# Partial sums of the middle token stages added in DRAM by POOL's transfers, rests copied out by ACT, seven-product blocks of 512 columns, first weight slots in other buffers

## Chip, cores and metric

One core of one Trainium2 chip (trn2). The metric is the device time of one execution in microseconds, from three executions of the kernel before: 2330.68 (median), 2330.60 and 2334.85.

## What is computed

The inputs are x (32 x 128 x 2048, fp32) and the weights of two layers of which the second follows the first. Cut to what matters:

```python
# layer 1: weight [2048, 2048] + low-rank part, quantised by groups of 128 to a 32-level codebook
lora_delta = lora_B @ lora_A * 0.5
normalized = (weight + lora_delta).reshape(2048, 16, 128) / exp(scale_log)
quantized  = cb[searchsorted((cb[:-1] + cb[1:]) * 0.5, normalized)]
w_eff      = (quantized * scale).reshape(2048, 2048) + lora_delta
y = x @ w_eff.T
# layer 2: a base matrix, a rank-16 part mixed by a softmax over 8 experts
result = y @ W_base.T + b_base
ax, probs = y @ A_w.T, softmax(y @ router_w.T)
mixed  = einsum(ax, cores, probs)
return x + result + mixed @ B_w.T * 2
```

The kernel never forms y. It multiplies w_eff with [W_base; A_w; router_w] first (2048 x 2072), and x with that product.

## The kernel before

The 16 blocks of 128 rows of the contraction are taken in four groups of four, g = 0 to 3. For each group there is a **weight stage**, in which TensorE multiplies the quantised weight with the wide second matrix and leaves the product in SBUF as a high and a low part (`gh`, `gl`, 2072 columns each), and then a **token stage**, in which all 32 tokens (t, tiles of 128 rows of x) are multiplied with it. Every fp32 factor is held as a rounded high part and a remainder, and each product is three matmuls (high x high, high x low, low x high). Beside all of it a background of quantisation "levels" for the later groups runs on ACT (masks `mk` and `mp`), DVE (`acc`) and POOL (`tm`, `pp`).

Four token stages add to the same 32 x 128 x 2072 result, which does not fit into SBUF. It lies in DRAM as `part`, one tile of 1,036 KB for each token, and three SBUF buffers `R.part[t % 3]` hold what is in work.

The change is in the **middle token stages, g = 1 and g = 2**. There tokens are taken in pairs p = 0 to 15. The first and the last pair are plain: for each token five "chunks" of 384, 384, 384, 512 and 408 columns, 12 matmuls each. The 14 pairs between are "mixed": the first `SW` = 448 columns of both halves of the result (`HX` = 1036 columns each) come from a scheme with seven products instead of eight (`prod` 1 to 7, 6 matmuls of `SW` columns each), and the remaining columns of each token are three "rest" units (12 matmuls of `REST` columns each). The thirteen units of a mixed pair run in this order:

```python
MIX = (("prod", 1), ("prod", 2), ("rest", 0, 0), ("rest", 0, 1), ("prod", 6), ("prod", 5), ("rest", 0, 2), ("prod", 7),
       ("prod", 3), ("rest", 1, 0), ("prod", 4), ("rest", 1, 1), ("rest", 1, 2))
```

Positions in a pair are counted by this list, 0 to 12 (`at` in the code). The products alternate between two PSUM banks (`unit_bank`), the rests go round four others. TensorE waits in `mul` until the unit that used its bank before has been taken out.

The generator `walk` yields all events in one order, and each engine's program picks its own from it, so the order of an engine's instructions is fixed by the places of the `yield`s; each engine then waits on semaphores alone. In the middle stages of the kernel before:

- SP (the queue of all transfers) loads the tokens' x (`load_x`, L872 to L883) at position 0 for both tokens of the next pair, loads each token's old partial sum from DRAM into `R.part[t % 3]` (`load_part`, L890) once the store of token t - 3 has landed (semaphores `po`), and stores it back (`store_part`, L901) when DVE has added the last unit of it. It is one queue: what waits holds up what stands behind.
- DVE takes every unit out of PSUM by adding it to the loaded buffer (`mul_added`, L1743 to L1761), which waits for the load (`pi`) once for each token.
- ACT rounds x to its high part (`split_x`, L1505) and POOL subtracts to get the low part (`split_x`, L2038), for the even token at position 5 and the odd token at position 7. POOL also forms the sums of x blocks for the next pair (`token_sums`, L2056 to L2061), which ACT rounds (L1517) and DVE finishes (L1769).
- The weights of the next weight stage come in small slots (`weight`, L852 to L870). The first six are asked for at position 6 of the last pair. Four of them lie in the `part` buffers, and wait for the last stores from these (`po`).

## Time and profile before

| | us |
|---|---|
| median of three executions | 2330.68 |
| the other two | 2330.60, 2334.85 |
| the profiled execution, its own time | 2334.6 |
| its span, first to last instruction | 2331.3 |
| PE busy in the span | 2252.6 (97%) |
| DVE / ACT / POOL busy | 1952.5 / 1495.4 / 1391.5 |
| mean granted TensorE clock | 0.992 |

The stages follow each other in the span like this: token stage g = 1 from 891.6 to 1244.5 us, weight stage g = 2 to 1426.9, token stage g = 2 to 1776.0, then the weight and token stage of g = 3. "Busy" of PE counts a matmul from its start to a modelled end, and consecutive matmuls overlap: the time that a matmul costs is read from the distance of two starts, not from its duration.

### The profile page before, as it was taken

What the parts mean: (1) busy time and instruction counts of PE and PEld (TensorE: products, weight loads), DVE (VectorE), ACT (ScalarE), POOL (GpSimd) and SP (SyncE); (2) the same over time, 40 slices, a digit from 0 to 9 for tenths busy, and PEclk for the clock granted to TensorE, in tenths of its full rate; (3) what the DMA queues carried; (4) which work ended last, traced back from release to release, by engine and by line L of the source; (5) the groups of instructions that cost most, each with busy time, mean ns of one, the idle gap of its engine ahead of it and who ended that gap; (6) DMA issues with size and microseconds to landing.
All of it is one profiled execution on the core that took longest, in us unless ns stands there. A gap on an engine that the chain in (4) does not pass through costs nothing.

```text
span 2331.3 us, 31903 instructions
## 1 busy us (share of the span) xinstructions
PE 2252.6 (97%) x11610; PEld 2061.2 (88%) x11610; DVE 1952.5 (84%) x2501; ACT 1495.4 (64%) x1962; POOL 1391.5 (60%) x902
## 2 busy tenths in 40 slices
PE   3989899999999999999999999999999999999999
PEld 2445479999999989999999989999999999999998
DVE  8999998889988977989997988999996766777676
ACT  7999978989877764666664865666663664121221
POOL 6888846669874545878775635988872132233331
PEclk9999999999999999999999999999999999999999
DMA  6787854444334334656664334566656666656454
GB/s 209 260 288 272 315 208 170 163 170 145 133 128 149 116 109 169 254 214 240 248 231 153 115 109 167 221 244 246 234 223 195 187 193 192 226 192 235 189 222 154
DMA packets 133233, 459.62 MB, mean 197 GB/s; under 512 B 14114, under 2 KB 66914, under 8 KB 96354
## 3 DMA queue, kind: packets, MB, share of 16 engines
q1 hardware_dynamic: 133076, 457.59, 56.1%
q8 instruction: 91, 1.49, 0.3%
q14 instruction: 66, 0.54, 0.1%
HBM read 306.41 MB, written 151.13 MB: 196 GB/s over the span
## 4 chain that ended last, share of the span: by engine, by line
PE 80%; DVE 8%; DMA 4%; ACT 3%; POOL 2%; issue 2%; SPq 0%; DVEq 0%; POOLq 0%; ACTq 0%
PE m L1228 6%; PE m L1227 6%; PE m L1229 6%; PE m L1179 5%; PE m L1180 5%; PE m L1181 5%; DVE acc L1701 5%; PE m L1120 5%; PE m L1334 4%; PE m L1336 4%; PE m L1335 4%; PE m L1294 3%; PE m L1293 3%; PE m L1295 3%; PE m L1284 3%; PE m L1285 2%
## 5 line engine op out<-in xcount | busy, mean ns | idle before, releaser
L1701 DVE SCALAR_TENSOR_TENSOR acc<-mk,dj,acc 128x1024 f32<-128x1024 uint8 x736 | 944.4, 1283 | 91.4 <-ACT mk L1449 73.2
L1449 ACT ACTIVATE mk<-wr,bj 128x1024 uint8<-128x1024 f32 x736 | 811.1, 1139 | 0.5 <-DVE acc L1701 0.4
L2014 POOL TENSOR_TENSOR pp<-pp,tm 128x1024 f32<-128x1024 f32 x184 | 456.9, 2483 | 22.9 <-POOL tm L2000 1.5
L2000 POOL TENSOR_SCALAR tm<-mp,dj 128x1024 f32<-128x1024 uint8 x192 | 225.8, 1177 | 219.8 <-ACT mp L1455 213.0
L1799 DVE TENSOR_TENSOR kl<-kw,kh 128x416 fp32r<-128x416 f32 (+3 forms) x310 | 240.5, 785 | 84.5 <-ACT kh L1484 83.5
L1484 ACT ACTIVATE kh<-kw 128x416 fp32r<-128x416 f32 (+3 forms) x310 | 169.1, 548 | 183.2 <-DMA kw<-in_wb 91.9
L1228 PE MATMUL m<-gl,xh 128*128 128x384 f32 (+2 forms) x800 | 280.9, 351 | 0.0
L1227 PE MATMUL m<-gh,xh 128*128 128x384 f32 (+2 forms) x800 | 280.6, 351 | 0.0
L1229 PE MATMUL m<-gh,xl 128*128 128x384 f32 (+2 forms) x800 | 279.9, 350 | 0.0
L1455 ACT ACTIVATE mp<-wr,bj 128x1024 uint8<-128x1024 f32 x224 | 255.0, 1139 | 13.7 <-POOL wr L1980 13.7
L1761 DVE TENSOR_TENSOR part<-m,part 128x448 f32<-128x448 f32 (+4 forms) x362 | 210.8, 593 | 34.1 <-PE m L1229 16.7
L1179 PE MATMUL m<-kh,wh 128*128 128x384 f32 (+2 forms) x624 | 219.3, 351 | 0.6 <-DVE part L1761 0.6
L1181 PE MATMUL m<-kh,wl 128*128 128x384 f32 (+2 forms) x624 | 218.6, 350 | 0.0
L1180 PE MATMUL m<-kl,wh 128*128 128x384 f32 (+2 forms) x624 | 218.6, 350 | 0.0
L1120 PE MATMUL m<-rows,wr 128*128 128x384 f32 (+2 forms) x560 | 208.3, 535 | 2.6 <-DMA rows<-in_wb 2.2
L1120 PEld LDWEIGHTS m<-rows,wr 128*128 128x128 f32 x560 | 112.5, 201 | 97.3 <-issue 51.5
L1840 DVE TENSOR_TENSOR part<-m,part 128x346 f32<-128x346 f32 (+1 forms) x272 | 137.1, 516 | 69.3 <-PE m L1336 36.0
L1334 PE MATMUL m<-op,pxh 128*128 128x346 f32 (+1 forms) x544 | 178.8, 329 | 0.0
L1335 PE MATMUL m<-op,pxh 128*128 128x346 f32 (+1 forms) x544 | 174.3, 320 | 0.0
L1293 PE MATMUL m<-gh,xh 128*128 128x392 f32 x504 | 171.8, 341 | 2.3 <-DVE part L1761 2.3
L1294 PE MATMUL m<-gl,xh 128*128 128x392 f32 x504 | 171.8, 341 | 0.0
L1295 PE MATMUL m<-gh,xl 128*128 128x392 f32 x504 | 171.4, 340 | 0.0
(249 smaller groups left out, 5140.8 us busy)
## 6 DMA issues: line engine op xcount, KB each, us to landing
part<-part SPq DMA_DIRECT2D x191, 1036.0 KB, 4.8
rows<-in_wb SPq DMA_DIRECT2D x61, 1036.0 KB, 4.8
out<-part SPq DMA_DIRECT2D x31, 1024.0 KB, 4.8
kw<-in_ws SPq DMA_DIRECT2D x128, 208.0 KB, 2.7
xw<-in_x SPq DMA_DIRECT2D x96, 256.0 KB, 5.1
kw<-in_wb SPq DMA_DIRECT2D x92, 192.0 KB, 2.4
wr<-in_w SPq DMA_DIRECT2D x32, 512.0 KB, 5.8
dl<-delta SPq DMA_DIRECT2D x30, 512.0 KB, 5.4
```

The costliest lines, as they stand in the source:

```text
L1120: done = e.matmul(R.m[c][:, 0:width(c)], R.wr[raw_of(q)][:, (t % 8) * 128:(t % 8 + 1) * 128], R.rows[r % 3][:, cols(c)], start=t == 0, sto ...
L1179: e.matmul(bank[:, 0:w], high, kh, start=t == 0, stop=False)
L1180: e.matmul(bank[:, 0:w], high, kl, start=False, stop=False)
L1181: done = e.matmul(bank[:, 0:w], low, kh, start=False, stop=t == NB - 1 and not own(b, c))
L1227: e.matmul(R.m[c][:, 0:w], xh, gh, start=k == 0, stop=False)
L1228: e.matmul(R.m[c][:, 0:w], xh, gl, start=False, stop=False)
L1229: done = e.matmul(R.m[c][:, 0:w], xl, gh, start=False, stop=stop and k == n - 1)
L1334: e.matmul(bank, high, oh, start=kp == 0 and n in (1, 2, 5), stop=False, skip_group_check=n in (3, 4, 6, 7))
L1335: e.matmul(bank, high, ol, start=False, stop=False, skip_group_check=n in (3, 4, 6, 7))
L1449: e.activation(R.mk[m % NM], w, ACT.Identity, bias=R.bj[:, j:j + 1], scale=GROW).then_inc(S["mk"], 1)
L1701: e.scalar_tensor_tensor(R.acc, R.mk[m % NM], R.dj[:, j:j + 1], R.acc, ALU.mult, ALU.add).then_inc(S["ac"], 1)
L2014: e.tensor_tensor(R.pp, first, R.tm[scaled_level(q, i)], ALU.add).then_inc(S["pp"], 1)
```

## The change

In the token stages g = 1 and g = 2:

1. **Partial sums.** `load_part` is gone, and `store_part` stays for g = 0 alone. A unit is now written into `R.part[t % 3]` by a copy, or, for the second and later product of the same target, added to what this pair has put there. When a token's last unit is out, POOL issues one transfer that adds the whole buffer to `part[t]` in DRAM (`add_part`; `accum_op=ALU.add`, rows in two pieces of 1036 elements). It stands at position 10 of the pair for the even token, and at position 1 of the next pair for the odd one. The first unit of token t waits until the transfer of token t - 3 has landed (semaphores `pa`).
2. **Who takes out.** ACT copies the rest units and chunks 0, 1, 2 (`mul_copied`); DVE takes out the products and chunks 3, 4 (`mul_evicted`).
3. **Low part of x.** For the odd tokens (beyond the first pair) it moves from POOL to DVE, and from position 7 to 10 (8 in plain pairs). The even token's x is asked for at position 8 of the pair before (`fetch_ahead`) instead of position 0 of the next.
4. **Columns.** `SW` goes from 448 to 512. The rests shrink from 392, 392 and 392 columns to 348, 348 and 352. To make room, the buffer `sf` of the x sums moves to the enlarged `las`.
5. **Weight slots.** For the weight stages g = 2 and g = 3 the first six slots, and slots 10 and 11, lie in `las`, in the four x buffers, and in freed places of the raw weights or `dl` (`GUESTS`). None of them waits for a transfer of partial sums.

The diff, cut to its core:

```diff
-GUEST = {4: 2, 5: 0}
-GUEST_LAST = {2: 0, 3: 1, 10: 0, 11: 1}
+GUESTS = {1: {4: "x2", 5: "x0"},
+          2: {0: "las", 1: "x0", 2: "x1", 3: "x2", 4: "sh", 5: "x3", 10: "las", 11: "sh"},
+          3: {0: "las", 1: "x0", 2: "x1", 3: "x2", 4: "sl", 5: "dl", 10: "sl", 11: "dl"}}
...
-SW = 448
+SW = 512
...
                 yield ("x_split", g, 2 * p + 3)
-                yield ("more", g, p)
...
-            if at == 7:
+            if at == (10 if mixed(p) else 8):
                 yield ("x_low", g, 2 * p + 3)
...
+        if at == (10 if mixed(p) else 6):
+            yield ("half_stored", g, p)
+        if p and at == 1:
+            yield ("pair_stored", g, p - 1)
+        if at == 8 and p + 2 < PAIRS:
+            yield ("fetch_ahead", g, 2 * p + 4)
...
-        elif s in GUEST:
-            e.wait_ge(S["mc"], x_released(g - 1, GUEST[s]))
+        place = GUESTS[g].get(s, "")
+        if place[:1] == "x":
+            e.wait_ge(S["mc"], x_released(g - 1, int(place[1])))
+        elif place == "las":
+            e.wait_ge(S["ql"], sums_count(g - 1, MIX_LAST))
+        elif place == "dl":
+            e.wait_ge(S["we"], NQ)
+        elif place:
+            e.wait_ge(S["mc"], sums_free(g - 1))
...
-    def load_part(g, t):
-        if t < 3:
-            e.wait_ge(S["used"], NS * (g - 1) + RELEASED[t])
-        else:
-            e.wait_ge(S[f"po{t % 3}"], slot_round(g, t - 3))
-        e.dma_start(R.part[t % 3], part[t]).then_inc(S[f"pi{t % 3}"], 16)
...
+    def mul_copied(g, k):
+        p, kind, u, i = UNITS_OF[g][k]
+        t = 2 * p + u
+        part, bank = R.part[t % 3], (*R.m, R.pd)[unit_bank(UNITS_OF[g][k])]
+        if t >= 3 and k == token_units(g, t, True)[0]:
+            e.wait_ge(S[f"pa{t % 3}"], slot_round(g - 1, t - 3))
+        e.wait_ge(S["mc"], multiplied(g, k))
...
+        e.activation(to, of, ACT.Copy).then_inc(S["ea"], 1)
...
-    def mul_added(g, k):
+    def mul_evicted(g, k):
...
-        if k == first_unit(g, t, 0):
-            e.wait_ge(S[f"pi{t % 3}"], slot_round(g - 1, t))
+        if t >= 3 and k == token_units(g, t, False)[0]:
+            e.wait_ge(S[f"pa{t % 3}"], slot_round(g - 1, t - 3))
         e.wait_ge(S["mc"], multiplied(g, k))
...
+        if before is None:
+            e.tensor_copy(to, of).then_inc(S["ed"], 1)
+            return
+        wait_unit_evicted(e, S, g, before)
         e.tensor_tensor(to, of, to, ALU.add).then_inc(S["ed"], 1)
...
+    def add_part(g, t):
+        wait_unit_evicted(e, S, g, token_units(g, t, True)[-1])
+        wait_unit_evicted(e, S, g, token_units(g, t, False)[-1])
+        if g == 1:
+            e.wait_ge(S[f"po{t % 3}"], 16 * PER_SLOT[t % 3])
+        else:
+            e.wait_ge(S[f"pa{t % 3}"], slot_round(g - 2, t))
+        e.dma_start(part[t], R.part[t % 3], accum_op=ALU.add, max_dma_last_dim=4 * HX).then_inc(S[f"pa{t % 3}"], 16)
```

How the instructions move, at the places that matter. `m` and `pd` are PSUM banks, `part_98`, `part_99`, `part_100` the three SBUF buffers, `part` alone the tensor in DRAM, `xw_88`, `xw_89`, `xw_90`, `xw_172` the four x buffers.

POOL in a mixed pair of stage g = 1, before (the sums for the next pair, both low parts, and the levels `tm`, `pp`):

```order
L2056 TENSOR_TENSOR sf<-xw_89 128x256
L2057 TENSOR_TENSOR sf<-xw_88,xw_89 128x256
L2059 TENSOR_TENSOR sf<-sf,xw_88 128x256
L2061 TENSOR_TENSOR sf<-xw_88,sf 128x256
L2038 TENSOR_TENSOR xl_91<-xw_88,xh_94 128x512
L2038 TENSOR_TENSOR xl_92<-xw_89,xh_95 128x512
L2000 TENSOR_SCALAR tm_133<-mp_140,dj 128x1024
L2014 TENSOR_TENSOR pp<-pp,tm_133 128x1024
L2000 TENSOR_SCALAR tm_133<-mp_141,dj 128x1024
L2014 TENSOR_TENSOR pp<-pp,tm_133 128x1024
```

and the same pair in the changed kernel:

```order
L2105 TENSOR_TENSOR sf<-xw_89 128x256
L2106 TENSOR_TENSOR sf<-xw_88,xw_89 128x256
L2108 TENSOR_TENSOR sf<-sf,xw_88 128x256
L2110 TENSOR_TENSOR sf<-xw_88,sf 128x256
L2087 TENSOR_TENSOR xl_91<-xw_88,xh_94 128x512
L2049 TENSOR_SCALAR tm_133<-mp_140,dj 128x1024
L2063 TENSOR_TENSOR pp<-pp,tm_133 128x1024
L2119 DMA part<-part_98 128x2x1036
L2049 TENSOR_SCALAR tm_133<-mp_141,dj 128x1024
L2063 TENSOR_TENSOR pp<-pp,tm_133 128x1024
L2119 DMA part<-part_99 128x2x1036
```

One low part is gone from POOL, and two transfers stand among the levels, each behind waits for ACT's and DVE's last units of its token.

SP at the end of token stage g = 1, before: two stores stand ahead of the first weight slots (`kw_112` to `kw_115` lie in `part` buffers), and four of the six slots wait for stores that have landed:

```order
L901 DMA part<-part_98 128x2072 [waits s_ed]
L817 DMA wr_51<-in_w 128x1024 [waits s_mc,s_used]
L870 DMA kw_112<-in_wb 128x384 [waits d_po2]
L870 DMA kw_113<-in_wb 128x384 [waits d_po2]
L870 DMA kw_114<-in_wb 128x384 [waits d_po0]
L870 DMA kw_115<-in_wb 128x384 [waits d_po0]
L870 DMA xw_90<-in_wb 128x384 [waits s_mc]
L870 DMA xw_88<-in_wb 128x384 [waits s_mc]
L901 DMA part<-part_99 128x2072 [waits s_ed]
```

and in the changed kernel:

```order
L934 DMA xw_172<-in_x 128x512 [waits s_mc]
L863 DMA wr_51<-in_w 128x1024 [waits s_mc,s_used]
L921 DMA lasw_199<-in_wb 128x384 [waits s_ql]
L921 DMA xw_88<-in_wb 128x384 [waits s_mc]
L921 DMA xw_89<-in_wb 128x384 [waits s_mc]
L921 DMA xw_90<-in_wb 128x384 [waits s_mc]
L921 DMA shw_202<-in_wb 128x384 [waits s_mc]
L921 DMA xw_172<-in_wb 128x384 [waits s_mc]
L921 DMA kw_112<-in_wb 128x384 [waits d_pa2,s_used]
```

The first six slots wait only for units of TensorE or for the last x sums, and nothing of the partial sums stands in SP's queue.

## Rows read from the trace of the kernel before

**Rows 1.** The page, part 1: busy time, share of the span, instructions.

```profile
PE 2252.6 (97%) x11610; PEld 2061.2 (88%) x11610; DVE 1952.5 (84%) x2501; ACT 1495.4 (64%) x1962; POOL 1391.5 (60%) x902
```

**Rows 2.** Busy time by stretch: both middle token stages, the first 24 us after.

```profile
core 0: us, PE busy (x) PEld busy (x) DVE busy (x) ACT busy (x) POOL busy (x), PEclk, DMA share, GB/s
891.60:1244.50 352.90, 348.27 (x1838) 334.36 (x1838) 315.17 (x368) 216.57 (x226) 280.42 (x189) 1.00 0.62 226
1426.90:1776.00 349.10, 346.51 (x1838) 333.17 (x1837) 314.41 (x368) 215.15 (x225) 273.55 (x191) 1.00 0.61 226
1776.00:1800.00 24.00, 22.20 (x116) 21.00 (x116) 13.40 (x24) 9.20 (x20) 0.00 (x0) 1.00 0.81 214
```

**Rows 3.** Timeline of PE, first matmuls of units: start, duration, line, tiles, shape.

```profile
897.87 0.40 PE L1227 MATMUL m<-gh,xh 128*128 128x512 f32 x1
...
900.66 0.34 PE L1227 MATMUL m<-gh,xh 128*128 128x408 f32 x1
...
999.81 0.34 PE L1294 MATMUL m<-gl,xh 128*128 128x392 f32 x1
...
1002.33 0.36 PE L1284 MATMUL m<-gh,xh 128*128 128x448 f32 x1
...
1004.77 0.34 PE L1293 MATMUL m<-gh,xh 128*128 128x392 f32 x1
...
1009.03 0.36 PE L1284 MATMUL m<-th,sh 128*128 128x448 f32 x1
...
2041.31 0.32 PE L1335 MATMUL m<-op,pxh 128*128 128x346 f32 x1
...
2042.42 0.32 PE L1336 MATMUL m<-op,psl 128*128 128x346 f32 x1
```

**Rows 4.** Waits in 891.6:1244.5: total us, times, longest us.

```profile
ACT xh L1505 <- DMA xw<-in_x: 73.9, 12, 9.3
PE m L1284 <- DVE part L1761: 3.1, 5, 2.1
PE m L1293 <- DVE part L1761: 1.2, 1, 1.2
```

**Rows 5.** Busy time by stretch, around the longest of these waits of PE.

```profile
1035.00:1040.00 5.00, 2.93 (x11) 2.38 (x10) 4.15 (x7) 5.00 (x5) 4.85 (x5) 0.77 0.61 212
1040.00:1045.00 5.00, 5.00 (x25) 4.74 (x24) 4.31 (x7) 4.00 (x5) 4.63 (x6) 0.88 0.32 133
```

**Rows 6.** Timeline of SP and of DVE just before it.

```profile
1024.90 0.91 SPq L883 DMA_DIRECT2D xw<-in_x  x2
...
1033.40 1.29 DVE L1701 SCALAR_TENSOR_TENSOR acc<-mk,dj,acc 128x1024 f32<-128x1024 uint8 x1 [3.70 <-ACT mk L1449]
```

**Rows 7.** Groups of instructions by form: DVE and POOL in 891.6:1244.5.

```profile
L1761 DVE TENSOR_TENSOR part<-m,part 128x448 f32<-128x448 f32 x98 | 59.7, 617 | 5.7 <-PE m L1286 4.7
L1761 DVE TENSOR_TENSOR part<-m,part 128x392 f32<-128x392 f32 x63 | 35.1, 558 | 1.6 <-PE m L1295 1.5
L1761 DVE TENSOR_TENSOR part<-pd,part 128x392 f32<-128x392 f32 x21 | 11.7, 557 | 0.8 <-PE pd L1295 0.7
...
L2038 POOL TENSOR_TENSOR xl<-xw,xh 128x512 fp32r<-128x512 f32 x30 | 39.6, 1327 | 2.7 <-ACT xh L1505 1.3
```

**Rows 8.** The same view of the whole span: copies out of PSUM, DVE's low part.

```profile
L1741 DVE COPY part<-m 128x512 f32<-128x512 f32 x32 | 21.9, 684 | 1.7 <-PE m L1229 1.7
L1523 ACT ACTIVATE part<-m 128x384 f32<-128x384 f32 x96 | 46.6, 485 | 28.3 <-PE m L1229 28.0
L1873 DVE TENSOR_TENSOR xl<-xw,xh 128x512 fp32r<-128x512 f32 x32 | 38.9, 1215 | 6.0 <-ACT xh L1505 6.0
```

**Rows 9.** DMA in 891.6:1244.5: issues with us to landing; SP's own waits.

```profile
part<-part SPq DMA_DIRECT2D x61, 1036.0 KB, 4.8
...
SPq L890 <- DMA part<-part: 138.8, 29, 8.8
```

**Rows 10.** Timeline of SP and ACT at the end of stage g = 2.

```profile
1754.02 11.63 SPq L901 DMA_DIRECT2D part<-part  x2
1765.69 1.39 SPq L868 DMA_DIRECT2D kw<-in_ws  x2
...
1771.67 1.01 ACT L1484 ACTIVATE kh<-kw 128x408 fp32r<-128x408 f32 x2 [18.55 <-DMA kw<-in_ws]
```

More of the change, by code:

```diff
@@ L516, in first_at_home @@
 def first_at_home(g, s):
-    guests = {**GUEST, **(GUEST_LAST if g == LAST else {})}
-    return s not in guests and all(k in guests for k in range(s % RING, s, RING))
+    return s not in GUESTS[g] and all(k in GUESTS[g] for k in range(s % RING, s, RING))
 def wait_consumed(e, S, q):
@@ L600, in multiplied, with evicted, wait_unit_evicted @@
     return MC_BASE[g] + k + 1
-def added(g, k):
-    return ED_BASE[g] + k + 1
+def evicted(g, k):
+    scalar = by_scalar(UNITS_OF[g][k])
+    earlier = sum(by_scalar(u) == scalar for u in UNITS_OF[g][:k])
+    return ("ea", EA_BASE[g] + earlier + 1) if scalar else ("ed", ED_BASE[g] + earlier + 1)
+def wait_unit_evicted(e, S, g, k):
+    name, count = evicted(g, k)
+    e.wait_ge(S[name], count)
 def bank_before(g, k):
@@ L625, in sums_free, with x_low_on_vector, x_low_count, wait_x_low @@
     return multiplied(g, prod_unit(g, MIX_LAST, 3))
+def x_low_on_vector(g, t):
+    return g in MIXED and t % 2 == 1 and t > 1
+def x_low_count(g, t):
+    if g == 0:
+        return "xl", t + 1
+    if x_low_on_vector(g, t):
+        return "xm", (PAIRS - 1) * (g - 1) + t // 2
+    return "xl", NT + (PAIRS + 1) * (g - 1) + (t + 1 if t < 2 else t // 2 + 2)
+def wait_x_low(e, S, g, t):
+    name, count = x_low_count(g, t)
+    e.wait_ge(S[name], count)
 def x_buffer(g, t):
@@ L1177, in slot @@
             high, low = R.wh[high_of(q)][:, at], R.wl[raw_of(q)][:, at]
-            kl, kh = (k[:, 0:w] for k in R.ring(s)[1:])
+            kl, kh = (k[:, 0:w] for k in R.ring(g, s)[1:])
             e.matmul(bank[:, 0:w], high, kh, start=t == 0, stop=False)
@@ L1210, in last_slot @@
             high, low = R.wh[high_of(q)][:, r], R.wl[raw_of(q)][:, r]
-            kl, kh = (k[:, 0:2 * w] for k in R.ring(s, True)[1:])
+            kl, kh = (k[:, 0:2 * w] for k in R.ring(LAST, s)[1:])
             c0, c1 = max(o, a), min(o + 128, z)
@@ L1626, in scalar_program @@
                 weight(g + 1, 1)
+        elif what == "mul":
+            g, k = at
+            if k and by_scalar(UNITS_OF[g][k - 1]):
+                mul_copied(g, k - 1)
         elif what == "next_rounded":
@@ L1769, in token_sums_low, with x_low @@
         e.tensor_tensor(R.sl[g], R.sf, R.sh[g].bitcast(F32), ALU.subtract).then_inc(S["ql"], 1)
+    def x_low(g, t):
+        n, (xw, xl, xh) = GROUP[g] * 128, R.token(g, t)
+        e.wait_ge(S["xh"], NT * g + t + 1)
+        if mixed(t // 2):
+            e.wait_ge(S["qs"], 4 * sums_count(g, t // 2))
+        e.tensor_tensor(xl[:, 0:n], xw[:, 0:n], xh[:, 0:n].bitcast(F32), ALU.subtract).then_inc(S["xm"], 1)
     def spread(g, k):
@@ L1917, in vector_program @@
         elif what == "mul":
-            if at[1]:
-                mul_added(at[0], at[1] - 1)
+            g, k = at
+            if k and not by_scalar(UNITS_OF[g][k - 1]):
+                mul_evicted(g, k - 1)
         elif what == "spread":
@@ L1923, in vector_program @@
             token_sums_low(*at)
+        elif what == "x_low":
+            if x_low_on_vector(*at):
+                x_low(*at)
         elif what == "next_rounded":
@@ L2155, in gpsimd_program @@
                 clear()
-        elif what == "x_split" and at[0] and at[1] < 2 or what == "x_low":
+        elif what == "x_split" and at[0] and at[1] < 2 or what == "x_low" and not x_low_on_vector(*at):
             split_x(*at)
@@ L2163, in gpsimd_program @@
             token_sums(*at)
+        elif what == "half_stored":
+            add_part(at[0], 2 * at[1])
+        elif what == "pair_stored":
+            add_part(at[0], 2 * at[1] + 1)
         elif what == "close":
+            if at[0]:
+                add_part(at[0], NT - 1)
             if at[0] == 1:
```

157 lines of the change are left out of this document (72 added, 85 removed), and 2 rows, old and new, of the table COMPUTE.

## The prediction

> **What bounds the kernel now.** I read the page first: PE is busy 97% of the span, DVE 84% and POOL 60% [rows 1]. So TensorE's own work sets the time, and a change can save either columns of matmuls or the few places where PE waits. Then the view by stretch, for the two stages that are changed [rows 2]. In stage g = 1 (352.90 us) PE is idle 352.90 - 348.27 = 4.6 us, in stage g = 2 (349.10 us) 349.10 - 346.51 = 2.6 us, and in the 24 us after it 1.8 us. All of the idle time that this change can touch is thus 9.0 us, or 0.4% of 2331. DVE is busy 315 of 353 us there, POOL 280, ACT 217: DVE is the engine nearest to its limit, and PE's waits name it [rows 4]. A measurement can tell about 0.2% from no change, which is 4.7 us here.
>
> **Columns.** What a matmul costs is the distance of two starts. By the timeline [rows 3] 12 matmuls of 512 columns take 900.66 - 897.87 = 2.79 us (0.2325 each), 12 of 448 columns 2.44 us (0.2033), 14 and 24 of 392 columns 2.52 + 4.26 us (0.1784), and 7 of 346 columns 1.11 us (0.1586). Each mixed pair has 7 x 6 = 42 matmuls that go from 448 to 512, and 72 rest matmuls, of which 48 go from 392 to 348 and 24 to 352. The first cost 42 x 0.0292 = +1.23 us. For the others I lay a line through 392 and 346 (0.00043 us a column): 348 gives 0.1595, 352 gives 0.1612, so 48 x 0.0189 + 24 x 0.0172 = -1.32 us. The sum is -0.09 us a pair, and 28 pairs give **-2.6 us**. It is a small difference of two large terms. If all columns cost what 448 to 512 shows (0.00046), the 384 columns that a pair loses (42 x 64 = 2688 against 48 x 44 + 24 x 40 = 3072) save 0.175 us, or -4.9 us in all. If only the second stretch of 392 is taken (4.26 / 24 = 0.1775) the term turns to -0.6 us. I keep -4.9 and -0.6 as ends. The matmuls keep their number.
>
> **The one long stall.** The longest wait of PE in g = 1 is 2.1 us at 1035, on DVE [rows 4]. In that stretch the granted clock falls to 0.77, and stays at 0.88 in the next 5 us, where 25 matmuls start instead of some 28; of the 11 in the first stretch 2.93 us were used, where 448 columns at 0.2033 would take 2.24 [rows 5]. I put the slow clock at 0.7 + 0.5 = 1.2 us. The cause stands in [rows 6]: SP issued the x loads only at 1024.90, ACT waits for x in order and so makes no masks, and DVE waited 3.70 us for a mask. ACT spends 73.9 us of this stage on x [rows 4]. In the changed kernel no load or store of partial sums stands in SP's queue, and the even token's x is asked for five positions earlier. I take this stall away: **-3.3 us**. The odd token's x can't come earlier, since its buffer is freed only when the pair before ends; at 5 us to land it meets ACT at position 4, which PE reaches about 2 x 1.40 + 2 x 1.91 = 6.6 us into the pair.
>
> **The other idle time.** What is left is 4.6 - 2.1 + 2.6 + 1.8 = 6.9 us. DVE loses 98 adds of 448 and 84 of 392 columns, 59.7 + 35.1 + 11.7 = 106.5 us in a stage [rows 7]. It gets 98 evictions of 512 columns at about 0.684 (67.0 us) and 15 low parts at 1.215 (18.2 us) [rows 8]. That is -21 us of 315: its load falls from 89% to 84%. ACT gets 84 copies of about 350 columns, at no more than the 0.485 us of 384 columns [rows 8] 40.7 us, and 12 more in the plain pairs, 5.8 us: 217 + 47 = 264 of some 347 us, 76%, where it now waits more than that for x. Both stay below 90%, and rests have four banks in turn, so these edits are hidden. If the cover is gone PE waits for a rest's bank. At the end of a stage SP sat in two stores from 1754.02 and issued the first weight slots at 1765.69; ACT waited for them until 1771.67 [rows 10], and PE lost 1.8 us behind it. The new slots wait for none of this. I take three quarters of the 6.9 us away, **-5.2 us**, with ends 0 and -6.9.
>
> **What the change adds.** First, POOL's issues: 32 in a stage. No row shows a transfer issued by POOL. From below it is 0 where POOL would have waited anyway. From above: POOL is busy 280.4 us, loses 15 x 1.327 = 19.9 us [rows 7], and would be full in a stage of 347 us if an issue took (347 - 260.5) / 32 = 2.7 us. I take 1 to 2 us, which POOL's idle time hides. Second, the transfer's time T. A buffer was stored and then loaded again: two landings of 4.8 us one after the other, and SP waits 138.8 / 29 = 4.8 us for the first of them [rows 9], without one DVE wait for it among the waits of the stage. Now it is one transfer that must read, add and write. Its deadline is the same as before: issued after position 8 of a pair for the even token, needed when position 5 of the next is evicted. Between lie five products (6 x 0.2325 = 1.40 us) and five rests (12 x 0.16 = 1.92 us), 16.6 us. T lies between 4.8 us (a store alone) and, as the nearest row for reading and writing, 2 x 4.8 = 9.6 us; POOL's lateness of some 3 us comes on top. I expect it to be covered, and allow **+1.0 us** for new short waits.
>
> The traffic of a token was one read and one write in DRAM, and stays so, with the DMA share at 0.62 [rows 2]. The Trainium skill ("Collectives: The Full Stack", section "The bandwidth ceiling: the fold count and why AG ≠ RS ≠ AR") says of an adding transfer that the add itself costs nothing but that it needs two reads for each write, both on the same read ring, so that it runs at about half of a copy's rate. By that rule T would be near the 9.6 us and not near 4.8, and still inside the 16.6 us; no row here shows it.
>
> **Sum.** Against the profiled execution's own 2334.6 us (3.3 more than its span of 2331.3): -2.6 - 3.3 - 5.2 + 1.0 = -10.1, so 2324.5. This execution lies 3.9 us above the median of 2330.68, about what the stall at 1035 costs, and the other two may well not have it. By that the median would lose 6 to 7 us. Both ways I come to **2324.3 us**.
>
> **Rivals.**
> (A) *Nothing that can be told.* The stalls that I take away come back as others of the same size, since ACT, which ran free of PE, is now tied to it by a wait for each rest, and DVE's masks come behind ACT's copies. For it: the columns alone give only -2.6. Against it: DVE is relieved by 21 us a stage. Time: 2326 to 2335, centre 2329.
> (B) *The adding transfer is late; slower.* Place: the first product of the odd token, position 5. From the end of position 8 a period holds POOL's delay (3 us), T, one eviction (0.7 us) and the product at position 8 that needs the same bank (1.4 us). It exceeds the pair's 21.3 us from T = 16.2 us on, and then each us of T costs 1 us a pair, 28 us in all. With T = 17 it is +22 - 10 = +12, or 2343 us; with 18, +40, or 2371. For it: nothing shows the adder's speed, x and raw weights travel beside it. Against it: 16.2 is over three times 4.8.
> (C) *POOL becomes the bound; slower.* It decides from 2.7 us an issue. At 3.5 us POOL needs 260.5 + 112 = 372.5 us in g = 1 and 273.6 - 19.9 + 112 = 365.7 in g = 2, which is +19.6 and +16.6 against the spans before, so about 2366 us. Two waits stand before each issue as well, and levels, x sums and low parts queue behind them. The Trainium skill ("SBUF — State Buffer", section "Who interferes with whom") says that POOL writes the descriptors of its transfers itself and is locked out of its port while DVE runs an instruction in a two-port mode. What would make that come true is DVE's evictions, 98 a stage at 0.68 us; by that rule the issues would wait for them. But 684 ns for 512 columns [rows 8] is 1.34 ns a column, no faster than the two-source adds from PSUM (617 ns for 448, 1.38) [rows 7], so I give it no more than the chance of (C).
> (D) *The change doesn't do what it says* at the stage ends: the slot in the last x buffer waits for the stage's last unit, and the six loads stand in one queue. Then the 1.8 us stay, 2326 us, inside the forecast.
>
> **Chances.** Forecast 0.60 (2315 to 2327), (A) 0.20, (B) 0.08, (C) 0.12. Of the forecast 0.03 lies above 2326.0, and of (A) 0.03 above 2335.3, so faster by over 0.2% is 0.57, within 0.2% 0.03 + 0.17 = 0.20, slower 0.08 + 0.12 + 0.03 = 0.23. The range reaches down to the lower ends of the terms (-4.9 - 3.3 - 6.9 on 2330.7, 2315.6) and up over (A) to a mild (B), 2340.
>
> **What would show it.** Right: starts of 348 columns 0.16 us apart and of 512 0.2325; pair period near 21.3; no long PE wait on DVE in g = 1 and no clock below 0.95 there; ACT's wait for x far below 73.9 us; SP's first slot loads before 1760; POOL below 95% in both stages. Wrong: DVE or ACT waiting on the adding transfer (B); POOL full, with ACT or PE waiting for POOL's `tm`, `sf` or `xl` (C); stages no shorter than 350 us with many waits under 1 us (A).

## The result and the profile after

The changed kernel takes **2350.08 us** (median of 4 runs, 2346.51 to 2351.85) against 2332.12 us of the kernel before on the same chip (4 runs, 2330.6 to 2334.85). The ratio is **1.0073**, with a 95% interval of 1.0058 to 1.0088: slower by 0.7%. I had forecast 2324.3 us, and 2340 us was the upper end of my range. The profiled execution below took 2349.72 us, its span is 2347.6 us.

The page of the changed kernel, parts 1, 3 and 6 (issues: count, KB each, us to landing); it answers to [rows 1] and [rows 9]:

```profile
PE 2253.2 (96%) x11610; PEld 2027.8 (86%) x11610; DVE 1917.4 (82%) x2339; ACT 1571.9 (67%) x2154; POOL 1431.6 (61%) x936
...
q0 software_dynamic: 17408, 67.90, 16.2%
...
HBM read 238.51 MB, written 151.13 MB: 166 GB/s over the span
...
part<-part POOLq DMA_DIRECT2D x64, 1036.0 KB, 8.9
```

DVE was relieved as forecast (84% to 82%), ACT got its copies (64% to 67%), and an adding transfer lands after 8.9 us, inside my 4.8 to 9.6. The counter of HBM reads fell by 67.9 MB, from 306.41, which is exactly the 64 loads that went: what the adder reads of its target is not in that counter (it stands at the same 238.51 MB in `a_plain` below, where nothing is added).

Busy time by stretch in the changed kernel, for both middle stages, the 24 us after them, and 5 us around the longest wait; it answers to [rows 2, 5]:

```profile
core 0: us, PE busy (x) PEld busy (x) DVE busy (x) ACT busy (x) POOL busy (x), PEclk, DMA share, GB/s
889.80:1247.90 358.10, 346.71 (x1839) 316.50 (x1839) 295.21 (x288) 256.46 (x324) 295.43 (x203) 0.99 0.64 132
1429.50:1787.00 357.50, 347.70 (x1838) 316.48 (x1837) 294.38 (x287) 253.14 (x321) 291.60 (x201) 0.99 0.63 129
1787.00:1811.00 24.00, 20.05 (x95) 19.07 (x94) 9.75 (x17) 5.58 (x11) 2.30 (x7) 0.86 0.86 192
955.00:960.00 5.00, 3.52 (x12) 3.11 (x13) 4.27 (x6) 0.00 (x0) 4.71 (x4) 0.74 1.07 233
```

The stages are 5.2 and 8.4 us longer than before. PE's idle time in them went from 4.6 and 2.6 us to 11.4 and 9.8 us. No other engine is full: POOL stands at 82%, DVE at 82%. In the 24 us after, PE lost 4.0 us where it had lost 1.8, and the granted clock was 0.86.

The waits in 889.8:1247.9 of the changed kernel (total us, times, longest us); they answer to [rows 4]:

```profile
DVE acc L1739 <- ACT mk L1470: 38.6, 39, 3.4
...
PE m L1305 <- DVE part L1795: 6.9, 5, 3.7
DVE part L1795 <- DMA part<-part: 5.0, 1, 5.0
...
ACT xh L1526 <- DMA xw<-in_x: 2.7, 3, 1.1
...
PE m L1314 <- DVE part L1789: 2.2, 1, 2.2
PE m L1305 <- POOL xl L2087: 2.2, 1, 2.2
```

ACT's wait for x fell from 73.9 to 2.7 us as forecast. In its place stands one wait of DVE for an adding transfer, and behind it PE's longest wait. I followed that one back. Timeline of POOL, DVE and PE of the changed kernel (start, duration, line; in brackets the idle time before it and who ended it):

```profile
934.83 2.42 POOL L2021 TENSOR_TENSOR wr<-wr,dl 128x1024 f32<-128x1024 f32 x1
937.33 2.23 POOL L2029 TENSOR_TENSOR wr<-wr,rs 128x1024 f32<-128x1024 f32 x1
939.51 2.88 POOL L2068 TENSOR_TENSOR wr<-wr,sc 128x1024 f32<-128x1024 f32 x1
942.47 2.40 POOL L2075 TENSOR_TENSOR wr<-wr,dl 128x1024 f32<-128x1024 f32 x1
944.82 1.21 POOL L2119 DMA_DIRECT2D part<-part  x1
...
955.73 0.69 DVE L1795 COPY part<-m 128x512 f32<-128x512 f32 x1 [5.01 <-DMA part<-part]
...
956.48 0.50 PE L1305 MATMUL m<-gh,sh 128*128 128x512 f32 x1 [3.73 <-DVE part L1795]
```

The transfer of the first mixed pair's even token stands in POOL's order behind four operations on 128x1024, from 934.83 to 944.82 us, 10 us. It lands 10.9 us after its issue (the median is 8.9), DVE's copy into that buffer waits 5.0 us, PE 3.7 us, and the clock is then 0.74 for 5 us (last row of the stretches above). The second stage has the same wait, 4.9 us, up to 1493.9 us.

For the experiments I use two measures beside the median: the length of each middle stage (from the start of its first matmul to the start of its last), and the distance from the start of one mixed pair to the next. Both come from the starts of PE's matmuls in the timeline. In us, of the profiled executions:

```
                       stage g=1  stage g=2  all behind it   13 pair periods of g=1
before                   352.6      348.8       555.7        21.39 undisturbed; 22.92, 21.87, 21.39, 21.39, 22.03, 25.21 ... 22.37 ...
changed                  357.7      357.2       560.9        21.13 undisturbed; 25.21, 26.67, 21.86, 23.28, 21.13, 22.35 ...
```

So the columns gave more than forecast, 0.25 us a pair, and new stalls took it all back: mostly in the first four periods of each stage, where the second one (26.67, and 27.70 in g = 2) holds the wait shown above. A further 5.2 us were lost behind the second stage.

### The profile page after: what moved, and what is told of

Same layout as the page of the kernel before. It is cut to its first block, busy times and chain, and to the rows that moved or that the text cites. A ratio compares the mean times of both kernels' runs of the same rounds, so it can differ in the third digit from the quotient of the medians.

```text
span 2347.6 us, 31968 instructions
## 1 busy us (share of the span) xinstructions
PE 2253.2 (96%) x11610; PEld 2027.8 (86%) x11610; DVE 1917.4 (82%) x2339; ACT 1571.9 (67%) x2154; POOL 1431.6 (61%) x936
## 3 DMA queue, kind: packets, MB, share of 16 engines
q0 software_dynamic: 17408, 67.90, 16.2%
HBM read 238.51 MB, written 151.13 MB: 166 GB/s over the span
## 4 chain that ended last, share of the span: by engine, by line
PE 83%; DVE 5%; DMA 4%; ACT 4%; POOL 3%; issue 2%; POOLq 0%; DVEq 0%; SPq 0%; ACTq 0%
PE m L1141 7%; PE m L1249 6%; PE m L1248 6%; PE m L1250 6%; PE m L1200 5%; PE m L1201 5%; PE m L1202 5%; PE m L1355 4%; PE m L1357 4%; PE m L1356 4%; PE m L1305 3%; PE m L1307 3%; PE m L1306 3%; PE m L1314 3%; PE m L1316 3%; PE m L1315 3%
## 5 line engine op out<-in xcount | busy, mean ns | idle before, releaser
L2049 POOL TENSOR_SCALAR tm<-mp,dj 128x1024 f32<-128x1024 uint8 x192 | 231.6, 1207 | 221.1 <-ACT mp L1476 215.4
L1843 DVE TENSOR_TENSOR kl<-kw,kh 128x416 fp32r<-128x416 f32 (+3 forms) x302 | 234.4, 786 | 87.6 <-ACT kh L1505 86.3
L1200 PE MATMUL m<-kh,wh 128*128 128x384 f32 (+2 forms) x600 | 211.2, 352 | 0.0
L1202 PE MATMUL m<-kh,wl 128*128 128x384 f32 (+2 forms) x600 | 210.6, 351 | 0.0
L1201 PE MATMUL m<-kl,wh 128*128 128x384 f32 (+2 forms) x600 | 210.5, 351 | 0.0
L1314 PE MATMUL m<-gh,xh 128*128 128x348 f32 (+1 forms) x504 | 162.8, 323 | 3.0 <-DVE part L1789 3.0
L1316 PE MATMUL m<-gh,xl 128*128 128x348 f32 (+1 forms) x504 | 163.0, 323 | 0.0
L1315 PE MATMUL m<-gl,xh 128*128 128x348 f32 (+1 forms) x504 | 162.4, 322 | 0.0
L1248 PEld LDWEIGHTS m<-gh,xh 128*128 128x128 f32 x800 | 150.4, 188 | 7.4
```

The lines of the kernel that those rows point to most:

```text
L1200: e.matmul(bank[:, 0:w], high, kh, start=t == 0, stop=False)
L1201: e.matmul(bank[:, 0:w], high, kl, start=False, stop=False)
L1202: done = e.matmul(bank[:, 0:w], low, kh, start=False, stop=t == NB - 1 and not own(b, c))
L1248: e.matmul(R.m[c][:, 0:w], xh, gh, start=k == 0, stop=False)
```

## The experiments

Each ran beside the kernel before on one chip; its median there was 2331.39 us for the first four, 2330.86 for the next four, 2331.42 for three, and 2331.12 for the last. Ratios are against it. Four kernels leave the adding out (`a_sp_plain`, `a_plain`, `a_sp_twice`, `a_small_add`): each partial sum is overwritten by that of the next stage. The changed kernel itself ran only beside its own kernel before (2332.12), so where a difference to its 2350.08 us is given, the ratios may put it some 2 us lower.

### Columns: wide ones in the kernel before, narrow ones in the changed

`b_sw512`, on the kernel before (the buffers of the sums are laid out as in the changed one):

```
-SW = 448
+SW = 512
```

> The kernel before with nothing but the 512 columns (and the x sums in the enlarged las). An undisturbed mixed pair takes 21.385 us before and 21.13 us after the change, so if that difference comes from the columns alone, 28 pairs give -7.1 us, and this kernel stands at 2325 us, or at about 2328 if the wider sums at the stage's start cost it the 1.8 us a stage that the changed kernel loses before its first mixed pair. Rival: the pair is shorter because x and partial sums are no longer in SP's queue; then the pair stays at 21.3 to 21.4 us and the time at 2331 or above. My own term of the prediction (-2.6 us) would give 21.29 us a pair.

Measured: 2335.49 us, ratio 1.0019 (1.0010 to 1.0029). Pair periods are 21.13 us where undisturbed, so the columns do give 0.25 us a pair. But 9 of the 13 periods of g = 1 are disturbed, by 0.4 to 1.5 us.

`a_sw448`, on the changed kernel, is the reverse edit.

> The changed kernel with 448 columns again. Theory 'columns': the undisturbed pair returns to 21.385 us, +7.1 us, and the wait of PE for the low part of x at the stage's start (2.2 us twice) goes, since the four sums are narrower; the first pairs keep their waits for DVE: about 2353 us. Rival 'the wide products make DVE late' (evictions of 512 columns take 0.68 us where 448 took 0.62): the waits of PE for DVE in the first four pairs, 9.0 us in g = 1 and 7.5 in g = 2, shrink to the 4.3 and 2.2 of before, and the time falls below 2345.

Measured: 2349.68 us, ratio 1.0078 (1.0063 to 1.0093), the same as the changed kernel. The periods are 21.39 us again, and long ones stay (24.31, 24.48, 23.61 in g = 1), with DVE's wait for the transfer at 4.2 us. So what slows the changed kernel is not mainly its columns. But the equal times are in part chance: stage g = 1 is 3.5 us shorter than in the changed kernel, and the weight stage behind it takes 186.0 us instead of 182.0, which no run explains.

### The adding taken out: who issues, and what is transferred

`a_plain`, on the changed kernel: POOL's transfers become plain stores.

```
-e.dma_start(part[t], R.part[t % 3], accum_op=ALU.add, max_dma_last_dim=4 * HX)
+e.dma_start(part[t], R.part[t % 3], max_dma_last_dim=4 * HX)
```

> The changed kernel with POOL's transfers without the adding (left out), all else kept. It shows what the adder itself costs: transfers take 8.9 us to land now. Theory 'the adder is slow': 5 to 6 us to land, DVE's wait of 5.0 us falls to about 1.5, PE's long waits at pair 2 to nothing, -6 to -10 us, and the first weight slots of g = 3 come earlier: about 2340. Theory 'POOL's lateness': nearly the whole of 8.9 us is the way of a POOL transfer, it lands in 8 us or more, and the time stays within 3 us of 2350.

`a_sp_plain`: these plain stores are issued by SP, at the same places and with the same waits.

```
 def gpsimd_program(e, R, S, part):
-    def add_part(g, t): ...
 def sync_program(e, R, S, io, part, delta, out):
+    def add_part(g, t):
+        ...
+        e.dma_start(part[t], R.part[t % 3]).then_inc(S[f"pa{t % 3}"], 16)
```

> The changed kernel with the 64 transfers issued by SP as plain stores at the same places of the order; the adding of the partial sums in DRAM is left out. It takes from POOL 62 issues of 1.24 us and all lateness of the issue, and from the transfer the adder. Theory 'POOL's order makes the transfer late' (DVE waited 5.0 us for a transfer that POOL issued at 946.8, behind four 128x1024 operations): the wait of DVE for the transfer goes, with the PE wait of 3.7 us and the slow clock behind it, 5.5 us in g = 1 and 6.6 in g = 2, and POOL's relief helps the first pairs: 2330 to 2336. Rival 'ACT's copies tie the masks': DVE keeps its 39 waits for ACT's masks in g = 1 (38.6 us) and the time stays above 2340.

Measured: `a_plain` 2331.71 us (ratio 1.0004, 0.9994 to 1.0013), `a_sp_plain` 2324.26 us (0.9969, 0.9956 to 0.9981). So 2350.1 - 2331.7 = **18.4 us** (16 by the ratios) go with the adding and 2331.7 - 2324.3 = **7.4 us** with POOL as the issuer. `a_sp_plain` has ACT's copies tied to PE just as the changed kernel has, 38 waits of DVE for masks (30.9 us), and yet both stages at 346.9 us: those waits cost PE nothing.

`a_plain` still has POOL's late issue, and in stage g = 2 even its plain transfer comes too late: it is issued at 1474.80 behind the same four operations and lands 9.3 us later, the second period is 25.12 us, and that stage takes 351.7 us where g = 1 takes 348.5. DVE's timeline there:

```profile
1484.14 0.69 DVE L1795 COPY part<-m 128x512 f32<-128x512 f32 x1 [3.43 <-DMA part<-part]
```

The DMA view of 891:1236 of `a_plain` and then of the changed kernel (queue: packets, MB, share of 16 engines; issues with us to landing):

```profile
q0 software_dynamic: 8176, 31.89, 23.5%
...
part<-part POOLq DMA_DIRECT2D x31, 1036.0 KB, 4.8
xw<-in_x SPq DMA_DIRECT2D x29, 256.0 KB, 2.8
```

```profile
q0 software_dynamic: 7888, 30.77, 50.2%
...
part<-part POOLq DMA_DIRECT2D x30, 1036.0 KB, 8.8
xw<-in_x SPq DMA_DIRECT2D x28, 256.0 KB, 4.0
```

For the same bytes the adding transfer occupies the 16 engines 345 x 0.502 / 30 = 5.8 us instead of 345 x 0.235 / 31 = 2.6 us, lands after 8.8 us instead of 4.8, and the x loads beside it take 4.0 us instead of 2.8.

POOL's group of the issues in the same stretch, in `a_plain` and in the changed kernel (count, busy us, mean ns, idle before):

```profile
L2119 POOL DMA_DIRECT2D part<-part x31 | 23.9, 771 | 3.5 <-ACT part L1557 2.6 <-POOL pp L2063 0.9
```

```profile
L2119 POOL DMA_DIRECT2D part<-part x30 | 37.0, 1234 | 3.0 <-ACT part L1557 2.5 <-POOL pp L2063 0.4
```

An adding issue takes POOL 1.23 us, a plain one 0.77 us.

### Three edits of the changed kernel, and one of the kernel before

`a_late_last`: the last transfer of the second middle stage is issued behind the ninth slot of the last weight stage.

```
 elif what == "close":
-    if at[0]:
+    if at[0] == 1:
         add_part(at[0], NT - 1)
 elif what == "slot":
+    if at == (LAST, 9):
+        e.wait_ge(S["used"], NS * (LAST - 1) + 9)
+        add_part(LAST - 1, NT - 1)
```

> The changed kernel with one transfer moved: the adding transfer of the last token of the second middle stage is issued by POOL after the ninth weight slot of the last stage, not with the first slot loads. In the changed kernel's profile the first slot loads of the last stage took 4.4 us and were issued in the same microsecond as this transfer, ACT then waited 5.6 and 4.6 us for them, and everything after 1787 us is 5.2 us longer than before. Theory T (the adding transfers' own load on the DMA engines slows the loads beside them): the part after the second middle stage goes from 560.9 back to 556 to 557 us, about -4 us, 2346 us. Theory S (the slots' new buffers and what they wait for make the start of the last stage late): no change, within 1 us of 2350.

Measured: 2353.25 us, ratio 1.0095 (1.0080 to 1.0110). Both stages stayed (356.6, 356.8 us), the rest grew from 560.9 to 564.9 us. A miss of both theories' numbers: slots at home (in the `part` buffers) wait until the transfer out of that place has landed, so its delay is theirs: the moved transfer lands at 1808.3 us, SP issues the next slot load at 1808.39, and PE waits 4.7 us behind that.

`a_old_slots`: the first slots in the buffers of before.

```
-          2: {0: "las", 1: "x0", 2: "x1", 3: "x2", 4: "sh", 5: "x3", 10: "las", 11: "sh"},
-          3: {0: "las", 1: "x0", 2: "x1", 3: "x2", 4: "sl", 5: "dl", 10: "sl", 11: "dl"}}
+          2: {4: "x2", 5: "x0"},
+          3: {2: "sl", 3: "dl", 4: "x2", 5: "x0", 10: "sl", 11: "dl"}}
```

> The changed kernel with the first weight slots of the last two weight stages in the buffers of before. Theory S: the last 560.9 us become 556, -4 us, 2346 us, and the weight stage between the middle stages keeps its 182 us. Theory T: the last part keeps its 561 us or gets 1 to 3 us longer, since the slots at home now wait for the last adding transfers to land; 2350 to 2353 us.

Measured: 2363.40 us, ratio 1.0131 (1.0114 to 1.0148). The weight stage between went from 182.0 to 189.5 us, the rest from 560.9 to 566.4 us. With adding transfers the new places are needed; they are worth 13 us to this kernel.

`a_early`: each mixed pair's even token is sent two steps earlier in POOL's order.

```
-if at == (10 if mixed(p) else 6):
+if at == (8 if mixed(p) else 6):
     yield ("half_stored", g, p)
```

> The changed kernel with the even token's adding transfer two steps earlier in POOL's order, ahead of the level work of steps 8 and 9. Theory O (the order: POOL issues the transfer up to 10 us late behind up to four 128x1024 operations, and DVE's copy into that buffer then waits 5 us): DVE's two waits of 5.0 us for part<-part go, with PE's waits of 3.7 us and the slow clock behind them; 3 to 6 us less in each middle stage, 2340 to 2344 us. Theory D (the first pairs are held up by DVE's and ACT's masks and by loads beside the adder, the transfer's lateness only shows it): the 5.0 us waits go or shrink, but the stages lose 0 to 2 us each, 2347 to 2350 us; and POOL may now wait for the evictions, 0 to 1 us a pair, later masks behind it.

Measured: 2367.99 us, ratio 1.0159 (1.0143 to 1.0174), 18 us slower still. The pair periods say why this does not refute the theory: the second period did fall from 26.67 to 21.13 us, and DVE no longer waits for the transfer, but the fourth, ninth and tenth are now 25.49, 27.44 and 25.43 us. Timeline of POOL, DVE and PE of `a_early` in the longest of them:

```profile
1115.61 1.21 POOL L2119 DMA_DIRECT2D part<-part  x1 [4.54 <-issue]
1116.40 2.36 POOL L2068 TENSOR_TENSOR wr<-wr,sc 128x1024 f32<-128x1024 f32 x1
1118.30 1.63 POOL L2034 TENSOR_SCALAR pp<-mp,dj,cn 128x1024 f32<-128x1024 uint8 x1
1119.46 2.78 POOL L2075 TENSOR_TENSOR wr<-wr,dl 128x1024 f32<-128x1024 f32 x1
1121.79 1.54 POOL L2049 TENSOR_SCALAR tm<-mp,dj 128x1024 f32<-128x1024 uint8 x1
1123.48 2.62 POOL L2063 TENSOR_TENSOR pp<-pp,tm 128x1024 f32<-128x1024 f32 x1
...
1116.25 7.62 DVE L1813 TENSOR_TENSOR xl<-xw,xh 128x512 fp32r<-128x512 f32 x1
1123.80 0.68 DVE L1795 COPY part<-m 128x512 f32<-128x512 f32 x1
...
1124.62 0.77 PE L1305 MATMUL m<-gh,xh 128*128 128x512 f32 x1 [5.64 <-DVE part L1795]
```

DVE's split of x, two sources in SBUF, took 7.62 us. It begins during POOL's issue and ends only after four POOL operations that follow without a gap. In the two middle stages of `a_early` six of these splits take over 3 us (this one, one of 6.5 and four of 4.7), and each begins during such an issue. The group of this line in both kernels, `a_early` and then the changed one, in g = 1:

```profile
L1813 DVE TENSOR_TENSOR xl<-xw,xh 128x512 fp32r<-128x512 f32 x15 | 30.3, 2020 | 2.2 <-POOL sf L2110 2.2
```

```profile
L1813 DVE TENSOR_TENSOR xl<-xw,xh 128x512 fp32r<-128x512 f32 x15 | 19.1, 1274 | 2.1 <-POOL sf L2110 2.1
```

So where in POOL's order an issue stands also seems to decide which DVE operation it collides with, and PE waits behind that for the eviction. No run separates the issue from the POOL operations behind it.

`b_fetch_sw512`: the kernel before with columns of 512 (as in `b_sw512`), and x of the even token asked for a pair earlier.

```
+if at == 8 and p + 2 < PAIRS:
+    yield ("fetch_ahead", g, 2 * p + 4)
 ...
 elif what == "fetch":
-    if p + 1 < PAIRS:
-        load_x(g, 2 * p + 2)
-        load_x(g, 2 * p + 3)
+    if p == 0:
+        load_x(g, 2)
+    if p + 1 < PAIRS:
+        load_x(g, 2 * p + 3)
 ...
+elif what == "fetch_ahead":
+    load_x(*at)
```

> The kernel before with columns of 512 in the products and with the even token's x fetched a pair earlier; loads, stores and adds of the partial sums as before. Theory W (the long stall of the first middle stage at 1035 us comes from x arriving late at ACT, which holds a mask back): ACT's x wait of 73.9 us falls below 10 us, the long stall goes, the first middle stage is 348 to 351 us long instead of 353.9 with columns of 512 alone, 2330 to 2332 us. Theory V (DVE at 88 to 89 per cent is what makes the small waits, whatever x does): 0 to -1.5 us against 2335.5.

Measured: **2322.12 us** (2321.54 to 2322.45, 4 runs), ratio **0.9960** (0.9945 to 0.9975): faster than both kernels, by more than either theory gave it. Both stages take 346.1 us, and from the third on all periods are 21.13 or 21.14 us. The stretches of both stages and the waits of the first:

```profile
891.00:1237.10 346.10, 342.16 (x1837) 313.46 (x1836) 319.54 (x368) 216.34 (x225) 281.69 (x189) 1.00 0.63 231
1420.10:1766.20 346.10, 342.20 (x1837) 313.48 (x1836) 318.56 (x368) 215.36 (x225) 274.70 (x191) 1.00 0.61 228
```

```profile
ACT xh L1510 <- DMA xw<-in_x: 53.4, 12, 7.5
...
DVE acc L1706 <- ACT mk L1454: 3.2, 6, 1.1
...
PE m L1289 <- POOL xl L2043: 1.4, 1, 1.4
...
PE m L1232 <- DVE part L1766: 0.9, 1, 0.9
```

DVE is busy 319.54 of 346.1 us, 92%, with PE at 99%, so DVE's load by itself was not what disturbed the pairs. ACT still waits 53.4 us for x, not below 10 as I had expected. But DVE's wait for masks is 3.2 us, where [rows 6] had one of 3.70 us alone: what counts is not how long ACT waits, but whether a mask is late behind it.

### The two shares of the adding transfer apart

`a_sp_twice`: `a_sp_plain` with each store made twice, first to a tensor that nobody reads.

```
+e.dma_start(twin[t], R.part[t % 3]).then_inc(S[f"pa{t % 3}"], 16)
 e.dma_start(part[t], R.part[t % 3]).then_inc(S[f"pa{t % 3}"], 16)
```

> The kernel in which SP stores the partial sums plainly (adding left out), but with each store made twice: once to a second tensor that nobody reads, then to the partial sums, and the buffer is free when both are down. Each partial sum then costs about 2 x 2.6 us of all 16 DMA engines and lands some 8 to 10 us after its issue, as an adding transfer does (5.8 and 8.9 us), while POOL issues nothing. Theory T (what the adding costs is its load on the DMA engines and its late landing): 2334 to 2343 us, with DVE waiting for part<-part again and a longer last stage. Theory P (it costs only in connection with POOL, which issues it for 1.2 us in its place of a full order): 2324 to 2328 us.

Measured: 2328.91 us, ratio 0.9990 (0.9981 to 1.0000). The DMA view of 891:1236:

```profile
q1 hardware_dynamic: 15344, 80.06, 60.2%
...
twin<-part SPq DMA_DIRECT2D x31, 1036.0 KB, 4.0
part<-part SPq DMA_DIRECT2D x31, 1036.0 KB, 7.0
```

The DMA engines are nearly as full as in the changed kernel (60.2 against 50.2 + 12.7%), a buffer is free only 7.0 us after its issue, and both stages still take 346.9 us. That load and a landing of 7.0 us cost the stages nothing when SP issues; the changed kernel's 8.8 us were not reached. But the part behind the stages takes 561.2 us instead of 556.8, nearly the changed kernel's 560.9. The first home slots stand right behind the last stores in SP's queue: their first load lands 7.0 us after its issue instead of 4.9 (in `a_sp_plain`), and PE waits 3.8 us behind it.

`a_small_add`: `a_sp_plain` with an adding transfer of 128x128 issued by POOL at each old place, for which nobody waits.

```
+e.dma_start(small[t], R.idn, accum_op=ALU.add, max_dma_last_dim=256).then_inc(S["sa"], 16)
```

> The kernel in which SP stores the partial sums plainly (adding left out), with an adding transfer of 128x128 issued by POOL at each place of the changed kernel's adding transfer, after the same waits for the evictions. Nobody waits for it. It shows what POOL pays as issuer without the transfer's size. Theory P: issue of 1.0 to 1.3 us each and POOL's waits return most of the loss, 2334 to 2345 us. Theory T: 1 to 8 us above 2324.3, as with the plain transfers issued by POOL (2331.7), so 2325 to 2332 us.

Measured: 2331.97 us, ratio 1.0000 (0.9991 to 1.0010), 7.7 us above `a_sp_plain`, with 1239 ns an issue. Its stages take 349.8 and 349.7 us, and nearly all of the difference in them is the first period: 25.21 and 25.08 us, as in the changed kernel (25.21), instead of 22.33. The rows of this place, timeline of DVE in `a_sp_plain` and of POOL and DVE in the changed kernel, with the wait of PE behind each:

```profile
916.18 1.58 DVE L1821 TENSOR_TENSOR sl<-sf,sh 128x1024 fp32r<-128x1024 f32 x1
...
919.50 0.42 PE L1329 MATMUL m<-gh,xh 128*128 128x348 f32 x1 [0.81 <-DVE part L1804]
```

```profile
914.64 1.35 POOL L2119 DMA_DIRECT2D part<-part  x1
...
915.27 2.98 DVE L1806 TENSOR_TENSOR sl<-sf,sh 128x1024 fp32r<-128x1024 f32 x1
...
919.99 0.66 PE L1314 MATMUL m<-gh,xh 128*128 128x348 f32 x1 [2.22 <-DVE part L1789]
```

An issue of POOL starts at 914.64 us in the changed kernel, and DVE's split beside it takes 2.98 us instead of 1.58. The difference of 1.4 us arrives at PE whole (2.22 against 0.81). The other half of the longer period is the clock: in 920:924 the granted clock is 0.59 in the changed kernel and 1.00 in `a_sp_plain`, and the 12 matmuls behind the wait start 0.29 instead of 0.16 us apart. In `a_small_add` the split takes 2.97 us and PE waits 2.2 us at this place too.

`b_fetch`: the kernel before with the early fetch alone.

> The kernel before with one edit: the even token's x is fetched a pair earlier; columns of 448. Theory W (x's late arrival at ACT made the long stall and most small ones): the middle stages lose 2 to 4 us and 0 to 2 us, pairs 21.38 us undisturbed, 2325 to 2329 us. Theory V (only together with the wider columns, which make the pair shorter than what SP and DVE keep up with): within 1 us of 2331.

Measured: 2324.02 us, ratio 0.9967 (0.9956 to 0.9978). The stages take 347.0 and 347.4 us. 7.4 us, over three quarters of the 8.7 that `b_fetch_sw512` gains, come from one load a pair that is asked for earlier.

### One transfer moved

`a_early_one`: as `a_early`, but only for the first mixed pair, whose transfer stood behind the four operations.

```
-if at == (10 if mixed(p) else 6):
+if at == (6 if not mixed(p) else 8 if p == 1 else 10):
     yield ("half_stored", g, p)
```

> The changed kernel with a single adding transfer of each middle stage earlier in POOL's order: the even token's of the first mixed pair, ahead of two 128x1024 operations (2.88 + 2.40 us) that it stood behind; all others as in the changed kernel. If its lateness times its long landing made the two 5.0 us waits, and if what made the version with all of them earlier slow were the other transfers (issued beside DVE's two-operand splits, which then took up to 7.6 us), the second pair period falls from 26.67 and 27.70 us to 21.1 to 22 us, all others stay, and the time falls by 9 to 12 us to 2338 to 2341 us. If any earlier transfer costs as much elsewhere as it gives: 2347 to 2352 us.

Measured: **2335.20 us** (2333.93 to 2337.94, 10 runs), ratio 1.0020 (1.0010 to 1.0030): two of POOL's 936 instructions moved, and 14.9 of the 18 us that the change had lost are back (12 by the ratios 1.0073 and 1.0020, 16.2 between the spans of the two profiled executions). POOL's timeline there:

```profile
936.43 2.23 POOL L2029 TENSOR_TENSOR wr<-wr,rs 128x1024 f32<-128x1024 f32 x1
938.60 1.21 POOL L2119 DMA_DIRECT2D part<-part  x1
939.41 2.33 POOL L2068 TENSOR_TENSOR wr<-wr,sc 128x1024 f32<-128x1024 f32 x1
941.83 2.41 POOL L2075 TENSOR_TENSOR wr<-wr,dl 128x1024 f32<-128x1024 f32 x1
```

The second periods fell from 26.67 and 27.70 to 21.13 and 21.14 us, the fourth from 23.28 and 22.88 to 22.15 and 22.13 us, and the stages take 351.0 and 349.6 us. The adding transfers still land after 9.0 us. 2335.2 us is below the 2338 to 2341 expected: of the profiled executions 6.7 + 7.5 us come from the stages and 1.2 from what is behind them.

## Why the prediction was wrong

**Where it failed: the price of the adding transfers.** My step was "I expect it to be covered, and allow +1.0 us", on "POOL's lateness of some 3 us". T was right as a median: 8.9 us, near the nearest row's 9.6 (at the place that decided it was 10.9). By the rule that I quoted from the Trainium skill ("Collectives: The Full Stack", section "The bandwidth ceiling: the fold count and why AG ≠ RS ≠ AR") T had to be near 9.6 and not 4.8; the trace agrees (8.9 against a plain 4.8). What was wrong is the lateness: at the first mixed pair it was some 10 us, since normalising one tile and correcting another put four operations of 128x1024 in a row ahead of the issue. I had taken one small figure for every pair, where the deadline is missed by the worst. `a_sp_twice` shows that the load and a landing of 7.0 us alone were covered, as I said, and `a_early_one` that one late issue a stage cost most: 12 to 15 us.

**POOL's issues.** "Which POOL's idle time hides" was wrong too. The time was inside my 1 to 2 us (1.23), and POOL never was the bound (C), but at the start of a stage the issue falls beside a DVE split that PE waits for. `a_small_add` is 7.7 us slower than `a_sp_plain`, of which 5.6 stand in the first periods. That `a_plain` is 7.4 us slower is near this by chance: half of it is the late transfer of g = 2. I had costed POOL's time as a sum over the stage and not at the place.

**Rival (B)** named the right buffer and place: DVE waits for the transfer at a product of the odd token. Its price was wrong. I let it begin only at T = 16.2 us and then hit all 28 pairs; it hit one pair in each stage, because POOL's delay differs from pair to pair. Its own sum gives the size: by the timeline position 8 ended at 932.86 us, so the delay was 12.0, and 12.0 + 10.9 + 0.7 + 1.4 = 25.0 us is 3.9 above the undisturbed 21.1, where PE waited 3.7.

**Columns: -2.6, measured -7.1 on the pairs.** 21.13 against 21.38 us is 0.25 us in each of 28 pairs. By the timeline 512 columns are 0.2306 us apart (mean of 254; I had 0.2325), 348 columns 0.1587 (I had 0.1595). Such errors of 1% count in a small difference of large terms (and the end that I gave as -0.6 comes to -0.8 by its own numbers). And I left out a cost of the same edit: the sums that are made at the start of a stage are 1024 wide instead of 896. From the first chunk to the first mixed pair it takes 25.3 us in `b_fetch_sw512` and 23.1 in `b_fetch`, 2.2 us longer, in each stage. Of -7.1 that leaves -2.7, and the two kernels' medians differ by 1.9 (by 1.3 when each is taken against its own runs of before). That this is near my -2.6 is luck: two errors cancel.

**The long stall: right in cause.** -3.3 us for x arriving late: in `b_fetch` the early fetch alone removes it, with 25.21 falling to 21.39 us and no other edit. It also removes most of the small disturbances of g = 1 that I had booked under the other idle time, and gives 7.4 us in all.

**The other idle time: -5.2.** Not gained in the changed kernel. With SP as issuer and no adding (`a_sp_plain`) it all came to 2324.3 us, my forecast to the tenth, but that is luck, since it leaves the adding out and came by other terms: more from the pairs' columns, less from the end, where what is behind the second stage was 1.1 us longer than before and not shorter. That DVE at 89% was what disturbs PE, on which I built this term, is refuted by `b_fetch_sw512` (92% and undisturbed).

**Rival (A)** does not hold for the reason it gave: ACT's copies tied to PE did bring 39 waits for masks, and `a_sp_plain`, with 38 of them and stages of 346.9 us, shows them free.

**The end of stage g = 2.** I took its 1.8 us away and it lost 5.2 us more. The new slots were loaded early where they don't wait for transfers. But the home slots behind them still wait until the last partial sums have landed (SP 9.5 us at this place in the changed kernel), and these land later. `a_late_last` (+4.0 us there) shows that dependence, and `a_sp_twice` (+4.4) that slot loads also land later beside fuller stores.

Still open: what of the remaining 11 us between `a_early_one` and `a_sp_plain` belongs to which collision. In the profiled executions 6.9 of them stand in the stages, 4.0 of these in their first periods, where `a_small_add` has 5.6, and 3.0 behind the stages. No kernel tried the first pair's issue away from DVE's split.

## What to carry to other kernels

When work moves into another engine's queue, look at what stands ahead of it at every occurrence, and hold the worst, not the mean, against the deadline: here two of POOL's 936 instructions in the wrong place cost 12 to 15 us. A change in several parts should be tried part by part: the load asked for earlier was worth 7.4 us by itself on the kernel before, and was buried under the transfers. And moving an issue earlier is no gain by itself: it may fall beside an operation of the neighbour engine that the critical engine waits for.
